# Stacked queries of an attention kernel: one read a turn from a scratch in device memory in place of 16 transfers

## What is computed

```python
H, KVH, HD, WIN = 16, 4, 8, 32          # 16 query heads share 4 key heads, 8 numbers a head
def sdpa(q, k, v, mask):
    scores = jnp.einsum('bhqd,bhkd->bhqk', q, k) / np.sqrt(HD).astype(np.float32)
    scores = jnp.where(mask, scores, jnp.float32(-1e+30))
    probs = jax.nn.softmax(scores, axis=-1)
    return jnp.einsum('bhqk,bhkd->bhqd', probs, v)
...
x = x + global_latent_attn(rmsnorm(x, norm1_w), ...)   # q, k: rope, then rms-normalised; causal mask
x = x + local_gqa_attn(rmsnorm(x, norm2_w), ...)       # the same, but a key is seen by the next 32 rows alone
```

## Time and profile before

| | us |
|---|---|
| median of 3 runs | 1412.62 (1412.34 to 1413.05) |
| the profiled execution | 1413.18 |
| its span | 1411.1 |
| attention half ends, about | 648 |
| PE busy | 1191.2 |
| DVE busy | 987.1 |

### The profile page before, as it was taken

How to read it: one execution, slowest core, us unless ns; L and a number is a source line. 1 busy time by engine, 2 the same in 40 slices (tenths; PEclk the granted TensorE clock), 3 DMA queues, 4 the chain that set the end, 5 groups by cost and what they waited for, 6 DMA issues and landing times.

```text
span 1411.1 us, 37144 instructions
## 1 busy us (share of the span) xinstructions
PE 1191.2 (84%) x15602; PEld 703.9 (50%) x15602; DVE 987.1 (70%) x1573; ACT 822.1 (58%) x1218; POOL 447.1 (32%) x577
## 2 busy tenths in 40 slices
PE   3267778888888876775889999999999999999986
PEld 1223333334444444443566666666666666666652
DVE  5636567667585747577867788777787777877755
ACT  2177778788887554432555655566555665555641
POOL 1104030202012424455654343333433334333410
PEclk8578889999999989886999999999999999999997
DMA  3011110111101221211121111011110110101101
GB/s 94 5 39 40 41 38 21 28 26 22 31 21 35 49 50 40 46 23 45 25 60 30 25 29 25 21 25 27 26 25 21 25 32 22 25 21 25 32 6 60
DMA packets 35989, 45.16 MB, mean 32 GB/s; under 512 B 12240, under 2 KB 18288, under 8 KB 35824
## 3 DMA queue, kind: packets, MB, share of 16 engines
q1 hardware_dynamic: 35824, 42.79, 12.7%
HBM read 7.90 MB, written 2.10 MB: 7 GB/s over the span
## 4 chain that ended last, share of the span: by engine, by line
PE 46%; DVE 5%; issue 1%; ACT 1%; DVEq 0%; ACTq 0%
PE psum L1206 8%; PE psum L1342 7%; PE psum L1295 5%; PE psum L1226 4%; PE psum L1317 4%; PE psum L1281 4%; PE psum L1216 4%; PE psum L1368 3%; DVE ffn_neg_max L1691 2%; PE psum L1266 1%; PE psum L1303 1%; PE psum L1272 1%; ACT ffn_hn L1547 1%; PE psum L1334 1%; PE psum L1238 1%
## 5 line engine op out<-in xcount | busy, mean ns | idle before, releaser
L721 ACT ACTIVATE att_probs<-psum 128x1024 f32<-128x1024 f32 (+2 forms) x384 | 355.3, 992 | 157.9 <-PE psum L565 156.4
L1638 POOL TENSOR_TENSOR ffn_rot<-ffn_rot,ffn_rot_sin 128x512 f32<-128x512 f32 x128 | 160.2, 1274 | 382.9 <-DVE ffn_rot L1669 382.9
L609 PE MATMUL psum<-att_probs,att_v 128*32 128x256 f32 (+3 forms) x3712 | 212.7, 358 | 4.2 <-DVE att_probs L846 3.1
L565 PE MATMUL psum<-att_q_stack,att_k_parts 64*128 64x512 bf16 (+4 forms) x1280 | 147.5, 307 | 60.3 <-ACT att_probs L721 38.6
L846 DVE TENSOR_TENSOR att_probs<-att_probs,att_causal_mask 128x1024 f32<-128x1024 f32 (+1 forms) x80 | 86.6, 1090 | 115.3 <-ACT att_probs L721 115.3
L609 PEld LDWEIGHTS psum<-att_probs,att_v 128*32 128x32 f32 x3712 | 99.3, 114 | 75.6 <-issue 45.0
L565 PEld LDWEIGHTS psum<-att_q_stack,att_k_parts 64*128 64x128 bf16 x1280 | 44.9, 96 | 167.3 <-ACT att_probs L721 101.8
L488 POOL TENSOR_TENSOR att_rot<-att_qk 128x1280 f32<-128x1280 f32 x6 | 17.4, 2902 | 297.6 <-ACT att_qk L752 297.6
L1520 ACT ACTIVATE ffn_max_t<-psum 68x128 bf16<-68x128 bf16 x64 | 17.5, 273 | 151.4 <-PE psum L1254 151.2
L1527 ACT ACTIVATE ffn_probs<-psum 128x1024 f32<-128x1024 f32 x64 | 65.7, 1026 | 59.1 <-PE psum L1281 59.1
L468 POOL TENSOR_TENSOR att_probs<-att_probs,att_local_mask 128x480 f32<-128x480 f32 (+1 forms) x48 | 67.8, 1419 | 99.3 <-ACT att_probs L721 99.2
(11 more groups left out here) (217 smaller groups left out, 2508.5 us busy)
## 6 DMA issues: line engine op xcount, KB each, us to landing
ffn_v_back<-ffn_v SPq DMA_DIRECT2D x120, 130.0 KB, 2.3
att_q_stack<-att_q_high SPq DMA_DIRECT2D x192, 32.0 KB, 2.0
att_q_stack<-att_q_mid SPq DMA_DIRECT2D x192, 32.0 KB, 2.0
att_q_stack<-att_q_low SPq DMA_DIRECT2D x128, 32.0 KB, 2.0
xres<-in_hidden SPq DMA_DIRECT2D x4, 512.0 KB, 4.2
out<-ffn_qk_t SPq DMA_DIRECT2D x3, 512.0 KB, 3.2
tail_f_wqkv<-in_f_wqkv SPq DMA_DIRECT2D x1, 768.0 KB, 4.6
tail_space<-in_f_wqkv SPq DMA_DIRECT2D x1, 768.0 KB, 6.2
```

The source lines that it names most:

```text
L565: ins = T.matmul(psum[:, banks[i] + at:banks[i] + at + width], k_parts[rows, p % 3, j, kt * P:(kt + 1) * P], q_stack[rows, turn % 2, j, q0 ...
L609: ins = T.matmul(psum[32 * g:32 * g + V_PAD, (4 + cc) * BANK + lo - cc * BANK: (4 + cc) * BANK + hi - cc * BANK], v[:, p % 4, kt, g, shift ...
L721: act.activation(probs[:, n % E_BUFS, 2 * j:2 * j + 2, 0:width], ps2((step % 2) * 2).rearrange("p (h c) -> p h c", h=2)[:, :, 0:width], AC ...
L1638: steps.did(pool.tensor_tensor(out, out, halves(k.rot_sin[:, n % 2, :])[:, :, 1 - half, :], ALU.add), g["added"] if half else None)
```

## The change

Phase 0 keeps its 16 transfers a turn. They are now ordered by term first, and the first turn's wait for each part stands before the first transfer that needs it; DVE gives the signal for the mid part by itself. From phase 1 on, SyncE copies the parts of a whole phase to `q_rows`, a scratch in device memory, once for each term: 8 transfers of all 128 rows, 256 KB each (the **spread**). There each row of the parts stands 8 times, in the order of the stack. It waits for all 8 to land, and then each turn's stack is one read of 512 KB. PE's and ACT's waits are changed to fit the new counts.

```diff
--- before.py
+++ after.py
@@ -353,7 +353,8 @@
     qkv_in_psum, qk_copied, v_ready = sem("qkv_in_psum"), sem("qk_copied"), sem("v_ready")
     head_sq_ready, mean_sq_ready, head_root_ready = sem("head_sq"), sem("mean_sq_s"), sem("head_root")
     rnorm_ready, rot_ready = sem("rnorm_s"), sem("rot_ready")
-    k_split_ready, q_split_ready = sem("k_split"), sem("q_split")
+    k_split_ready, q_split_ready, q_spread = sem("k_split"), sem("q_split"), sem("q_spread")
+    q_rows = nc.dram_tensor("q_rows", (len(PHASES), GROUP, 2 * P, S), BF16, kind="Internal").ap()
     qt_in_psum, kt_in_psum, hi_ready, lo_ready = sem("qt_in_psum"), sem("kt_in_psum"), sem("hi_ready"), sem("lo_ready")
     gathered = [sem("gathered0"), sem("gathered1")]
     scores_done, exp_done, pv_done = sem("scores"), sem("exp"), sem("pv")
@@ -433,6 +434,12 @@
     def add_gated(engine, c, b, signal=None):
         gated_add(engine, c, tail, keep, b, signal)
 
+    def gather(engine, turn, j, term):
+        p, r = divmod(turn, GROUP)
+        row = r * P // GROUP + 2 * j * HEAD_DIM
+        engine.dma_start(q_stack[term::TERMS, turn % 2, j, :],
+                         q_parts[term // PARTS][row:row + 2 * HEAD_DIM, p % 2, :]).then_inc(gathered[turn % 2], 16)
+
     with nc.Block() as block:
 
         @block.sync
@@ -445,18 +452,32 @@
                     sp.dma_start(*early.pop(0)).then_inc(tail.prefetched, 16)
                 p, r = divmod(turn, GROUP)
                 slot = turn % 2
+                if p == 0:
+                    if turn >= 2:
+                        sp.wait_ge(scores_done, STEPS * (last_unit[turn - 2] + 1))
+                    for term in range(TERMS):
+                        if turn == 0 and term == 0:
+                            sp.wait_ge(hi_ready, 1)
+                        if turn == 0 and term in (PARTS, 2 * PARTS):
+                            sp.wait_ge(q_split_ready, term // PARTS)
+                        for j in range(2):
+                            gather(sp, turn, j, term)
+                    continue
                 if r == 0:
-                    sp.wait_ge(hi_ready, 2 * p + 1)
-                    sp.wait_ge(q_split_ready, p + 1)
-                if turn >= 2:
-                    sp.wait_ge(scores_done, STEPS * (last_unit[turn - 2] + 1))
-                for j in range(2):
-                    rows = slice(r * P // GROUP + 2 * j * HEAD_DIM, r * P // GROUP + (2 * j + 2) * HEAD_DIM)
+                    by_term = q_rows[p].rearrange("r (x c) s -> (r x) c s", c=TERMS)
                     for term in range(TERMS):
-                        sp.dma_start(q_stack[term::TERMS, slot, j, :],
-                                     q_parts[term // PARTS][rows, p % 2, :]).then_inc(gathered[slot], 16)
-
-        PER_GATHER = 16 * 2 * TERMS
+                        if term == 0:
+                            sp.wait_ge(hi_ready, 2 * p + 1)
+                        if term in (PARTS, 2 * PARTS):
+                            sp.wait_ge(q_split_ready, 2 * p + term // PARTS)
+                        sp.dma_start(by_term[:, term], q_parts[term // PARTS][:, p % 2, :]).then_inc(q_spread, 16)
+                    sp.wait_ge(q_spread, 16 * TERMS * p)
+                sp.wait_ge(scores_done, STEPS * (last_unit[turn - 2] + 1))
+                sp.dma_start(q_stack[:, slot], q_rows[p, r].rearrange("(j x) s -> x j s", j=2)).then_inc(gathered[slot], 16)
+
+        def gathers_of(turn):
+
+            return sum(16 * 2 * TERMS if other < GROUP else 16 for other in range(turn % 2, turn + 1, 2))
 
         @block.gpsimd
         def _(pool):
@@ -548,7 +569,7 @@
                 turn = turn_of[n]
                 step = n * STEPS + j
                 if n == first_unit[turn] and j == 0:
-                    pe.wait_ge(gathered[turn % 2], PER_GATHER * (turn // 2 + 1))
+                    pe.wait_ge(gathered[turn % 2], gathers_of(turn))
                     if r == 0:
                         pe.wait_ge(hi_ready, 2 * (p + 1))
                         pe.wait_ge(lo_ready, 2 * (p + 1))
@@ -766,9 +787,11 @@
                     inverse_root(root[:], mean_sq[:], head_root_ready)
                 for p in qkv_due("q_hi", n):
                     act.wait_ge(qt_in_psum, p + 1)
-                    if p >= 2:
-                        for turn in (GROUP * (p - 1) - 2, GROUP * (p - 1) - 1):
-                            act.wait_ge(gathered[turn % 2], PER_GATHER * (turn // 2 + 1))
+                    if p == 2:
+                        for turn in (GROUP - 2, GROUP - 1):
+                            act.wait_ge(gathered[turn % 2], gathers_of(turn))
+                    if p > 2:
+                        act.wait_ge(q_spread, 16 * TERMS * (p - 2))
                     c.did(act.activation(q_parts[0][:, p % 2], side, ACT.Copy), hi_ready)
                 for p in qkv_due("k_hi", n):
                     act.wait_ge(kt_in_psum, p + 1)
@@ -952,7 +975,7 @@
                     high, mid, low = (part[:, p % 2] for part in q_parts)
                     c.did(V.tensor_tensor(q_rest, side, high, ALU.subtract), lo_ready)
                     c.settle()
-                    c.did(V.tensor_copy(mid, q_rest))
+                    c.did(V.tensor_copy(mid, q_rest), q_split_ready)
                     c.settle()
                     c.did(V.tensor_tensor(low, q_rest, mid, ALU.subtract), q_split_ready)
                 for p in qkv_due("k_lo", n):
```

## The result

| | before | after |
|---|---|---|
| median, us | 1412.48 (4 runs) | 1390.41 (1389.58 to 1392.13, 4 runs) |
| span of the profiled execution, us | 1411.1 | 1388.7 |
| mean granted clock of PE | 0.933 | 0.936 |
| MB moved by DMA | 45.16 | 59.79 |

The changed kernel takes 22.1 us less, a ratio of 0.9845 (95% interval 0.9828 to 0.9862). The forecast was 26.5 us less. A second set of five runs of the changed kernel gave 1390.15 against 1413.19.

What follows compares the result with a forecast made beforehand. No engine was full; the gather of stacked queries limited the local phases, not the global ones. Terms 3.3 + 1.9 + 3.0 + 11.5 + 2.3 + 4.5 = 26.5 us; 1413.2 - 26.5 - 0.6 gave 1386, range 1374 to 1401.

Steps and rivals of the forecast that it cites:

- Phase 0: Start of phase 0: high transfers no longer wait for the low part, 3.3 us gained.
- Phase 1: Start of phase 1: spread and read end 13.7 us after the high part is ready, 1.9 us gained (0.7 to 3.6).
- The rest of phases 1 to 3: Starts of phases 2 to 4: split ready tens of us ahead, no wait before, so 0 gained.
- Phase 4: 441 to 485 us: 7.0 us of gather waits go, but PE meets DVE's chain; 3.0 us gained (2.5 to 5).
- Phase 5: 485.4 to 530.5 us: 8.6 of waits plus 4 of clock, less 1.1 for smaller waits; 11.5 us gained (9 to 13).
- Phase 6: 530.5 to 559.7 us: DVE's packed chain moves up but is not shortened, so 0 gained.
- 559.7 to 582.3: Up to phase 7's first turn: a new 5.3 us wait replaces one of 1.5; 2.3 us gained (0.5 to 6).
- 582.3 to 605: Phase 7, from its first turn: the 4.0 us wait before turn 29 goes, clock effects shift; 4.5 us gained (2 to 7).
- 605 to 648: Given as 605 to 640 us: 3.7 us on the gather, but DVE's own chain ends there; 0 gained (up to 3.7).
- The feed-forward half: After attention: the change doesn't touch it, so it was to last as long as before.
- other waits take the rest: Rival: DVE waits behind the gather's in local stages, only phase 5's waits pay back; 14 us gained, 1399, chance 0.17.
- The slow scratch: Rival: slow spread makes phase starts wait longer; mild case 1400 us, chance 0.06; slower than before, 1420, chance 0.05.

Runs made afterwards that it cites:

- the run with the delay: The changed kernel with 14 more semaphore clears on each engine between attention and feed-forward halves, about 1 us: 1387.20 us, ratio 0.9824.

## Why the prediction was right, and where it was short

The direction, the mechanism and the range held: 1390.4 us against 1386 (1374 to 1401). By its terms, predicted and in the first profile:

- **Phase 0**, 3.3: 3.4. PE starts at 74.1 instead of 77.5.
- **Phase 1**, 1.9: 3.0. The spread and the read took 12.4 us instead of 13.7, which is this difference. The writes ran faster than the rows of before allowed, and a fixed part of 3 to 3.7 us, of which the sum had 1.6, made up for most of it; that the two errors nearly cancel is luck.
- **The rest of phases 1 to 3**, 0: 0.1.
- **Phase 4**, 3.0: 4.0 in both profiles of this kernel, but 1.2 in the run with the delay. The 7.0 us on the gather went, and 5.6 us of other waits came, 3.1 of them for DVE, as forecast, and 2.5 for ScalarE. PE's waits in phase 4 after (435.4 to 474.9 us):

```profile
PE psum L581 <- ACT att_probs L742: 2.5, 2, 2.2
PE psum L562 <- DVE xs L885: 2.2, 1, 2.2
PE psum L703 <- DVE tail_space L880: 2.1, 1, 2.1
```

Before there had been 1.8 us on L862 beside the gather and none of the others. So waits gave 1.4 us. The other 2.7 are the clock, 0.96 for 0.88, at which PE's matmuls are busy 32.0 us for 34.6; in the run with the delay the clock was 0.84, they took 36.1 us, and phase 4 was 42.1 us long. The sum had nothing for the clock here, since DVE was to be the limit; that the size came out near is in part luck.

- **Phase 5**, 11.5: 7.0. This is the step that failed, "8.6 + 4 - 1.1". The 8.6 us of waits went. The smaller waits, 1.9 us for ScalarE and DVE in the trace of before, became 4.0 in the first profile, 2.1 more, where 1.1 had been left. They are the first two rows (485.4 to 530.5 us before) and the last two (474.9 to 513 after):

```profile
PE psum L560 <- ACT att_probs L721: 1.0, 2, 0.9
PE psum L541 <- DVE att_k_parts L962: 0.9, 1, 0.9
PE psum L581 <- ACT att_probs L742: 2.9, 5, 1.6
PE psum L562 <- DVE att_k_parts L985: 1.1, 1, 1.1
```

The 4 us of clock did not come in the first profile (0.87) and came for the most part in the second (0.95, phase 5 of 35.3 us, a gain of 9.8).

- **Phase 6**, 0: -0.7, at a clock of 0.77 for 0.88 before, and 0.1 in the second profile at 0.82. The starts of phases 5 and 6 had no wait on the scratch. Phase 6's spread was issued at 493.2 us and its read at 503.1, for a turn that began at 512.9: a slack of some 6 us, where the prediction had under 2.
- **559.7 to 582.3**, 2.3: 3.2. The new wait at phase 7 was 4.0 us instead of 5.3, again the shorter spread.
- **582.3 to 605**, 4.5: 4.5. The clock there is 0.91 instead of 0.85.
- **605 to 648**, 0: 0.6. DVE's own chain ends there, as forecast, with a wait of 8.7 us on L1066 in place of 4.9.
- **The feed-forward half**, as long as before: 2.8 us longer in the profile. The run of before with a delay shows the same loss without the change, so that it belongs to the execution that was profiled.

These sum to 22.3 us (3.4 + 3.0 + 0.1 + 4.0 + 7.0 - 0.7 + 3.2 + 4.5 + 0.6 - 2.8), against 22.4 between the two spans. Of the missing 4.2 us, 4.5 are phase 5, 2.8 the feed-forward half and 0.7 phase 6, and the shorter spread, phase 4 and the end gave some 4 back.

Of the signs named beforehand, these came: no wait on the stacked queries inside a phase, waits of 2.6 and 4.0 us at phases 1 and 7 (3 to 4 and some 5 were named), reads that land in 3.6 us, none on the scratch at phases 5 and 6, the attention half 25.1 us shorter. PE's waits on DVE were larger in phases 4 and 7, as named, but not in phase 6. Two signs did not come: the granted clock over the local phases hardly moved, 0.86 before and 0.87 after (up in phase 4, down in 5 and 6), and the feed-forward half was not as long as before.

Of the rivals, "other waits take the rest" is what happened in part: ScalarE's and DVE's waits took 2.1 us in phase 5. The slow scratch did not happen: its 2.1 MB took 8.7 us in all at phase 1, 241 GB/s. The Trainium skill's warning about rows at large power-of-two pitches (DMA: Bandwidth & Descriptors, Latency and other measured facts) did not bear on rows 16 KB apart: at its 103 GB/s the spread would have taken 20 us.

What stays open is what makes a low stretch of the clock last 3.4 us in one execution and 10.3 in another of the same program, and with it whether phases 4 and 5 together take about 74.6 or 77.4 us.

## What to carry to other kernels

A gather of many small transfers costs its issues: 16 of 32 KB at 0.63 us on one queue are 10 us, where one read of the same 512 KB lands in 3.6, and it holds the engine once a turn is shorter than that. Going through device memory is cheap where the data is ready early, and it puts two landings on the path where the data is ready late; there, write first what the first reader needs, and read it before writing the rest (2.5 us at the two places here). Put the clock that a stage's waits seem to cost into the range and not into the forecast: of phase 5's 4 us nothing came in one profile and about 3 in the other. And profile a kernel twice before explaining a difference of 3 us in one stage.

## What was not expected of the hardware

The writes to device memory were faster than any row of before: a second 2.1 MB added 5.0 us, 420 GB/s, and both spreads moved some 370 GB/s at full share, where the rows of before gave 309 at most. Moving 14.6 MB more (59.79 against 45.16) shows in PE's waits at two phase starts alone. The same instructions give stages of distinct lengths, phase 5 with 35.3 or 38.1 us and phase 4 with 39.3 or 42.1, by how long the granted clock stays at its lower level; and with 1 us of delay between the halves five runs of the changed kernel spread over 11 us (1382.0 to 1393.1), while the median of the kernel before moved by 0.4.
